# Transposes in groups of eight: TensorE's order of work in a masked attention layer, taken in steps of two units

## The chip, the cores and the metric

The kernel runs on one core of a Trainium2 chip. The time is the device time of one execution in microseconds; lower is better. Before the change it is 4194.33 us, the median of three runs (4191.17 to 4195.89 us).

## What is computed

Sixteen samples of 1024 rows by 512 columns go through one attention layer with an adjacency mask and a residual. The mask is the same for all samples and heads.

```python
h = jnp.maximum(_layernorm(x, axis=-1), 0.0)
q = (x @ Wq + bq).reshape(b, n, H, HD)      # x is h here; H = 8, HD = 64
k = (x @ Wk + bk).reshape(b, n, H, HD)
v = (x @ Wv + bv).reshape(b, n, H, HD)
scores = jnp.einsum('bihd,bjhd->bhij', q, k) / jnp.sqrt(jnp.float32(HD))
mask = jnp.where(adj == 0, jnp.float32(-1000000000.0), jnp.float32(0.0))
scores = scores + mask[None, None, :, :]
weights = jax.nn.softmax(scores, axis=-1)
out = jnp.einsum('bhij,bjhd->bihd', weights, v)
x = x + out                                  # residual, heads side by side
```

## The kernel before

**Units.** All five instruction streams are written out by hand, and semaphores join them. One sample has 8 heads and 8 blocks of 128 query rows. Its attention is cut into 128 units (`UNITS`), 64 pairs of them to 64 blocks of scores (`SBLOCKS`). A group `g` is one head with half of its query rows (four row blocks, `GB`), and the eight units of a group are its eight blocks `j` of 128 keys. For each unit `u`:

- TensorE turns four 128x128 pieces of the probabilities into one of two PSUM buffers `T` (`turn_probs`, L525). The buffer is `u % 2`.
- ScalarE copies `T` to the high part of `pT` (`probs_hi`, L633), and VectorE subtracts that copy from `T` to make the low part (`probs_low`, L796). `pT` has three buffers (`PT`). When `probs_low` is done, semaphore `p_lo` rises.
- TensorE contracts both parts with the values (`contract`, two matmuls of 512 columns, L538) into the PSUM tile `O`, which gathers over the eight units of a group. It follows its transposes by two units (`LAG = 2`).

**Scores.** On every even unit TensorE also computes a block of scores (`score`, four matmuls, L513 and L514) into one of two PSUM buffers `S`, five blocks ahead (`LEAD = 5`). VectorE adds the mask and takes the row minimum (`shift`, L790); ScalarE takes the exponential one block later (`exponential`, L641).

**The rest.** On the third unit of a group (`u % NB == LAG`, NB = 8) the group before is finished: ScalarE has copied `O` to `oT` (`copy_out`, L617), TensorE turns it into the PSUM tile `misc` (`turn_out`, L546), ScalarE copies it out (`copy_y`, L624), GpSimd scales it and adds the residual. Further work stands at numbered units (`fill`): twelve matmuls for half a projection of q or k, in two halves of six (`project_qk`, L483, at 4, 6, 8, 9, 12, 14, 16 and 17 of each 32 units), twelve for a block of the values (`project_v`, L496, at 121, 123 to 127, and 0 and 1 of the next sample), four transposes of the normalised input (`turn_h`, L462, at 83, 85, 87, 88, 91, 92, 95, 96). All of them use the one PSUM bank `misc`, which ScalarE or VectorE empties: `evacuate_qk` (L654), `bias_v` (L783), `h_high` (L669) and `h_low` (L762).

**Order on each engine.** Each engine takes its stream in the order in which it is written. ScalarE's order for unit `u` is: `copy_out` if `u % 8 == 1`, `probs_hi(u)`, the exponential if `u` is even, `copy_y` if `u % 8 == 2`, `v_high`, `evacuate_qk`, `high` (L664, the high parts of q and k, one and two units after the evacuation), `h_high`. VectorE's order is: the reciprocal (L806), `h_low`, `probs_low(u)`, `shift` of this pair's score block if `u` is even, `bias_v`, `low_q` (L772), the statistics. So on VectorE the `shift` of a pair stands between `probs_low` of its two units.

**Waits of `turn_probs`.** Unit `u` needs its PSUM buffer free, so its first transpose waits until `probs_low(u - 2)` is done. `contract(u)` waits for `probs_low(u)`.

Of the kernel before, what the change touches and what calls it, by code (L numbers as in the profile page):

```python
# [41 lines left out]
UNITS = GROUPS * NB  # L42
# [8 lines left out]
LAG = 2  # L51
# [30 lines left out]
def some(n):  # L82

    return not (isinstance(n, int) and n <= 0)


def adj_preln_kernel(nc, x, adj, Wq, bq, Wk, bk, Wv, bv, out):
    with ExitStack() as ctx:
# [98 lines left out]
        def before(b, slot, is_y, last):  # L187

            uses = []
            for s in range(slot + 1):
                if s in V_AT and not (last and s >= V_FROM):
                    nxt, j = V_AT[s]
                    uses.append((s, False, v_biased, NB * (b + nxt) + j + 1))
                if s in QK_START and not (last and QK_START[s][0] == PAIRS - 1):
                    p, k = QK_START[s]
                    uses.append((s, False, qk_evac, 4 * (PAIRS * b + p + 1) + k + 1))
                if s in HT_AT and not last:
                    uses.append((s, False, h_lo, NB * (b + 1) + HT_AT[s] + 1))  # L200
                if s % NB == LAG and some(GROUPS * b + s // NB):
                    uses.append((s, True, y_copied, GROUPS * b + s // NB))
            at = [n for n, use in enumerate(uses) if use[:2] == (slot, is_y)][0]
            if at == 0:
                return v_biased, NB * b + V_EARLY
            return uses[at - 1][2:]
# [248 lines left out]
        def _(pe):  # L455
            def turn_h(b, t, free=None, bank=misc):

                pe.wait_ge(ln_done, NB * b + t + 1)
                if free:
                    pe.wait_ge(*free)  # L460
                for c in range(C):
                    mm = pe.transpose(bank[:, c * P:(c + 1) * P], x_tile(b, t)[:, c * P:(c + 1) * P], ident[:])  # L462
                mm.then_inc(h_turned, 1)

            def project_qk(b, p, k, part, free=None, bank=misc[:]):


                w, half = 1 - k % 2, k // 2
                pair = PAIRS * b + p
                cols = slice(half * HALF, (half + 1) * HALF)  # L470
                if part == 0:
                    pe.wait_ge(h_lo, NB * (b + p // PAIRS) + GB * (half + 1))
                    if some(pair):
                        pe.wait_ge(wqk_in, 16 * pair)
                    else:
                        pe.wait_ge(w0_split, 2 if k else 1)
                    if free:
                        pe.wait_ge(*free)
                parts = [(c, wl, hl) for c in range(C) for wl, hl in ((0, 0), (0, 1), (1, 0))]
                count = len(parts) // 2  # L480
                for n in range(part * count, (part + 1) * count):
                    c, wl, hl = parts[n]
                    mm = pe.matmul(bank, wqk[:, w, c, wl, :], hT[:, hl, c, cols],  # L483
                                   start=n == 0, stop=n == len(parts) - 1)
                if part == 1:
                    mm.then_inc(qk_mm, 1)

            def project_v(b, j, free, bank=misc[:]):

                pe.wait_ge(h_lo, NB * (b + 1))  # L490
                pe.wait_ge(*free)
                if isinstance(b, int) and b == 0:
                    pe.wait_ge(wv_split, 1)
                parts = [(c, wl, hl) for c in range(C) for wl, hl in ((0, 0), (1, 0), (0, 1))]
                for n, (c, wl, hl) in enumerate(parts):
                    mm = pe.matmul(bank, hT[:, hl, c, j * P:(j + 1) * P], wv[:, wl, c, :],  # L496
                                   start=n == 0, stop=n == len(parts) - 1)
                mm.then_inc(v_mm, 1)

            def score(b, s):  # L500

                n = SBLOCKS * b + s
                q, k = qk_buffers(s // 16, (s // 8) % 2)
                i = s % NB
                pair = PAIRS * b + s // 16
                pe.wait_ge(q_low, 4 * pair + 3 + (s // 8) % 2)
                pe.wait_ge(k_copied, 64 * (pair + 1))
                if some(n - 1):
                    pe.wait_ge(exped, n - 1)
                for half in range(2):  # L510
                    cols = slice(half * HALF, (half + 1) * HALF)
                    dst = S[:, s % 2, cols]
                    pe.matmul(dst, q[:, i * P:(i + 1) * P], k[:, 0, cols], start=True, stop=False)  # L513
                    mm = pe.matmul(dst, q[:, i * P:(i + 1) * P], k[:, 1, cols], start=False, stop=True)  # L514
                mm.then_inc(scored, 1)

            def turn_probs(b, u):

                n, g, j = UNITS * b + u, u // NB, u % NB
                if j == 0:  # L520
                    pe.wait_ge(exped, GB * (GROUPS * b + g + 1))
                if some(n - 1):
                    pe.wait_ge(p_lo, n - 1)
                for i in range(GB):
                    mm = pe.transpose(T[:, u % 2, i * P:(i + 1) * P],  # L525
                                      probs[:, (GB * g + i) % RING, j * P:(j + 1) * P], ident[:])
                mm.then_inc(turned, 1)

            def contract(b, u):

                n, g, j, head = UNITS * b + u, u // NB, u % NB, u // (2 * NB)
                if g == 0:
                    pe.wait_ge(v_ready, NB * b + j + 1)
                if j == 0 and some(GROUPS * b + g):
                    pe.wait_ge(o_copied, GROUPS * b + g)
                pe.wait_ge(p_lo, n + 1)
                for part in range(2):
                    mm = pe.matmul(O[:], vs[:, j, head, :], pT[:, u % PT, part, :],  # L538
                                   start=(j == 0 and part == 0), stop=(j == NB - 1 and part == 1))
                mm.then_inc(contracted, 1)  # L540

            def turn_out(b, g, free):
                pe.wait_ge(o_copied, GROUPS * b + g + 1)
                pe.wait_ge(*free)
                for i in range(GB):
                    mm = pe.transpose(misc[:, i * P:(i + 1) * P], oT[:, i * P:(i + 1) * P], ident[:])  # L546
                mm.then_inc(o_turned, 1)

            def score_ahead(b, u, last):
                s = u // 2 + LEAD  # L550
                if u % 2 == 0 and s < SBLOCKS:
                    score(b, s)
                if u % 2 == 0 and s >= SBLOCKS and not last:
                    score(b + 1, s - SBLOCKS)

            def fill(b, u, last):
                if u in V_AT and not (last and u >= V_FROM):
                    nxt, j = V_AT[u]
                    project_v(b + nxt, j, before(b, u, False, last))
                if u in QK_START and not (last and QK_START[u][0] == PAIRS - 1):  # L560
                    p, k = QK_START[u]
                    project_qk(b, p + 1, k, 0, before(b, u, False, last))
                if u in QK_AT and not (last and QK_AT[u][0] == PAIRS - 1):
                    p, k = QK_AT[u]
                    project_qk(b, p + 1, k, 1)
                if u in HT_AT and not last:
                    turn_h(b + 1, HT_AT[u], before(b, u, False, last))
# [10 lines left out]
                score(0, s)  # L578

            def body(b, first=False, last=False):  # L580
                for u in range(UNITS):
                    if u % NB == LAG:


                        turn_probs(b, u)
                        score_ahead(b, u, last)
                        contract(b, u - LAG)
                        if u == LAG and not first:
                            turn_out(b - 1, GROUPS - 1, before(b, u, True, last))
                        if u > LAG:  # L590
                            turn_out(b, u // NB - 1, before(b, u, True, last))
                        continue
                    if u >= LAG:
                        contract(b, u - LAG)
                    elif not first:
                        contract(b - 1, UNITS - LAG + u)
                    turn_probs(b, u)
                    score_ahead(b, u, last)
                    fill(b, u, last)

            body(0, first=True)
            with pe.Fori(1, B - 1) as b:
# [290 lines left out]
```

## Time and profile before

| | us |
|---|---|
| median of three runs | 4194.33 |
| lowest, highest | 4191.17, 4195.89 |
| span of the profiled execution | 4186.6 |
| TensorE matmul busy | 4080.4 (97%) |
| VectorE busy | 3120.0 (75%) |
| ScalarE busy | 3149.6 (75%) |
| GpSimd busy | 1287.4 (31%) |

The profile is of one execution. Its span runs from the first to the last instruction. A matmul is named by the line that issues it, and its end is modelled, because matmuls overlap: a matmul of 512 columns is shown as about 0.39 us long, while the next one starts 0.23 us after it. Where a stretch is priced below, the distance between starts is used. An idle time in square brackets is that of the engine just before the instruction, with what ended it.

### The profile page before, as it was taken

Reading aid. Unit: us, or ns where it says so; the run is one execution under the profiler, and the core shown is the slowest. Engines: PE = TensorE matmul, PEld = TensorE weight load, DVE = VectorE, ACT = ScalarE, POOL = GpSimd, SP = SyncE. Lnnn points to the kernel's source line nnn. Section 1 sums busy time; section 2 is a strip of 40 time slices with the busy share of each in tenths; the row PEclk is TensorE's granted clock in tenths of the full one; section 3 lists DMA queues with packets and bytes.
Section 4 is the critical chain, followed back from the end, with each engine's and each line's share of the span. In section 5 each row is a group of like instructions: output and inputs, shape, how many; then the busy total and the mean of one; then the engine's idle time right before and its main releaser. Section 6 shows DMA issues by size and latency. Waiting matters only on the chain.

```text
span 4186.6 us, 77847 instructions
## 1 busy us (share of the span) xinstructions
PE 4080.4 (97%) x22528; PEld 3370.6 (81%) x22528; DVE 3120.0 (75%) x5128; ACT 3149.6 (75%) x5642; POOL 1287.4 (31%) x1665
## 2 busy tenths in 40 slices
PE   7999999999999999999999999999999999999998
PEld 6888888888787887878878788788887888888887
DVE  6877868778687786777867677676777768767677
ACT  5877868778687786867868688686886868868687
POOL 4233332333323333223333233332332322333222
PEclk9999999999999999999999999999999999999999
DMA  5221212212222221122212122121221212212111
GB/s 176 72 73 56 81 48 75 66 57 83 61 60 67 65 77 59 59 67 76 66 59 71 54 76 66 59 79 47 76 72 54 82 48 71 83 44 83 46 51 31
DMA packets 219598, 282.56 MB, mean 67 GB/s; under 512 B 12305, under 2 KB 143377, under 8 KB 210577
## 3 DMA queue, kind: packets, MB, share of 16 engines
q1 hardware_dynamic: 219152, 277.14, 21.9%
q8 instruction: 217, 3.56, 0.4%
q14 instruction: 229, 1.87, 0.2%
HBM read 172.23 MB, written 37.75 MB: 50 GB/s over the span
## 4 chain that ended last, share of the span: by engine, by line
PE 89%; DVE 4%; issue 3%; ACT 2%; DMA 1%; POOL 1%; DVEq 0%; SPq 0%; POOLq 0%; ACTq 0%
PE O L538 21%; PE T L525 19%; PE misc L483 17%; PE S L513 10%; PE S L514 10%; PE misc L496 8%; PE misc L546 3%; DVE pT L796 2%; PE misc L462 1%; ACT pT L633 1%; DVE qA L772 1%; DMA xln<-in_x 1%; ACT qA L664 1%; DVE S L790 1%; DVE hT L762 0%
## 5 line engine op out<-in xcount | busy, mean ns | idle before, releaser
L796 DVE TENSOR_TENSOR pT<-T,pT 128x512 fp32r<-128x512 f32 x2048 | 1412.4, 690 | 831.1 <-ACT pT L633 808.8
L633 ACT CAST pT<-T 128x512 fp32r<-128x512 f32 x2048 | 1192.7, 589 | 711.0 <-PE T L525 676.1
L538 PE MATMUL O<-pT,vs 128*128 128x512 f32 x4096 | 1366.0, 415 | 60.0 <-DVE pT L796 46.0
L790 DVE CUSTOM_DVE_ANT_0 S<-S,mask 128x1024 f32<-128x1024 f32 x1024 | 1252.3, 1223 | 5.9 <-PE S L514 4.3
L525 PEld LDWEIGHTS T<-ident,probs 128*128 128x128 f32 x8192 | 1013.9, 140 | 258.4 <-ACT probs L641 0.3
L525 PE MATMUL T<-ident,probs 128*128 128x128 f32 x8192 | 1210.1, 272 | 0.0
L641 ACT ACTIVATE probs<-S,negmax 128x1024 f32<-128x1024 f32 x1024 | 1152.6, 1126 | 8.5 <-DVE negmax L790 5.3
L538 PEld LDWEIGHTS O<-pT,vs 128*128 128x128 f32 x4096 | 690.9, 189 | 178.2 <-DVE pT L796 70.4
L483 PE MATMUL misc<-hT,wqk 128*128 128x512 f32 x3036 | 789.1, 395 | 0.0
L483 PEld LDWEIGHTS misc<-hT,wqk 128*128 128x128 f32 x3036 | 560.6, 188 | 120.3
L400 POOL TENSOR_TENSOR yparts<-yparts 128x256 f32<-128x256 f32 x256 | 188.7, 737 | 1043.9 <-ACT yparts L624 1043.2
L513 PE MATMUL S<-kA,qA 128*128 128x512 f32 x1024 | 447.2, 437 | 3.9 <-ACT probs L641 3.2
L513 PE MATMUL S<-kB,qB 128*128 128x512 f32 x1024 | 447.0, 436 | 0.0
L514 PE MATMUL S<-kA,qA 128*128 128x512 f32 x1024 | 403.3, 394 | 0.0
L514 PE MATMUL S<-kB,qB 128*128 128x512 f32 x1024 | 402.3, 393 | 0.0
L496 PE MATMUL misc<-wv,hT 128*128 128x512 f32 x1476 | 363.8, 395 | 0.4 <-issue 0.4
L377 POOL TENSOR_TENSOR vs<-proj,vs 128x512 fp32r<-128x512 f32 x128 | 168.2, 1314 | 543.4 <-ACT vs L679 543.4
L496 PEld LDWEIGHTS misc<-wv,hT 128*128 128x128 f32 x1476 | 271.2, 188 | 65.8 <-issue 6.5
L654 ACT ACTIVATE proj<-misc,bqk 128x512 f32<-128x512 f32 x253 | 174.4, 689 | 182.7 <-PE misc L483 182.7
L390 POOL TENSOR_TENSOR kA<-proj,kA 64x512 fp32r<-64x512 f32 x128 | 164.5, 1285 | 474.9 <-ACT kB L664 474.9
L513 PEld LDWEIGHTS S<-kA,qA 128*128 128x128 f32 x1024 | 193.9, 189 | 27.2 <-issue 5.7
L514 PEld LDWEIGHTS S<-kA,qA 128*128 128x128 f32 x1024 | 195.2, 191 | 21.4
(68 smaller groups left out, 3333.0 us busy)
## 6 DMA issues: line engine op xcount, KB each, us to landing
wqk<-wqk_split SPq DMA_DIRECT2D x63, 1024.0 KB, 7.0
xln<-in_x SPq DMA_DIRECT2D x240, 256.0 KB, 3.7
xres<-in_x SPq DMA_DIRECT2D x66, 512.0 KB, 3.7
kA<-kA SPq DMA_DIRECT2D x128, 256.0 KB, 3.2
kB<-kB SPq DMA_DIRECT2D x128, 256.0 KB, 3.7
out<-xres SPq DMA_DIRECT2D x64, 512.0 KB, 3.2
probs<-in_adj SPq DMA_DIRECT2D x4, 1024.0 KB, 5.1
wqk_split<-vs SPq DMA_DIRECT2D x3, 1024.0 KB, 11.0
```

Source lines behind the costliest of these rows:

```text
L400: gp.tensor_tensor(y, y, yparts[:, :, 1], ALU.add).then_inc(y_summed, 1)
L483: mm = pe.matmul(bank, wqk[:, w, c, wl, :], hT[:, hl, c, cols], start=n == 0, stop=n == len(parts) - 1)
L496: mm = pe.matmul(bank, hT[:, hl, c, j * P:(j + 1) * P], wv[:, wl, c, :], start=n == 0, stop=n == len(parts) - 1)
L513: pe.matmul(dst, q[:, i * P:(i + 1) * P], k[:, 0, cols], start=True, stop=False)
L514: mm = pe.matmul(dst, q[:, i * P:(i + 1) * P], k[:, 1, cols], start=False, stop=True)
L525: mm = pe.transpose(T[:, u % 2, i * P:(i + 1) * P], probs[:, (GB * g + i) % RING, j * P:(j + 1) * P], ident[:])
L538: mm = pe.matmul(O[:], vs[:, j, head, :], pT[:, u % PT, part, :], start=(j == 0 and part == 0), stop=(j == NB - 1 and part == 1))
L633: act.copy(pT[:, u % PT, 0, :], T[:, u % 2, :]).then_inc(p_hi, 1)
L641: act.activation(probs[:, s % RING, :], S[:, s % 2, :], ACT.Exp, bias=negmax[:, s % RING:s % RING + 1], scale=-1.0, accum_out=rowsum[:, s ...
L654: act.activation(proj[:, k % 2], bank, ACT.Identity, bias=bqk[:, w, p % PAIRS:p % PAIRS + 1], scale=-SCALE if w == 0 else 1.0).then_inc(qk ...
L790: dve.tensor_tensor_reduce(S[:, s % 2, :], S[:, s % 2, :], mask[:, s % NB, :], 1.0, 3.0e38, ALU.add, ALU.min, negmax[:, s % RING:s % RING ...
L796: dve.tensor_tensor(pT[:, u % PT, 1, :], T[:, u % 2, :], pT[:, u % PT, 0, :].bitcast(F32), ALU.subtract).then_inc(p_lo, 1)
```

## The change

Only the order of TensorE's stream in the main loop changes, by two units at a time. In a step of units `u` and `u + 1`, both `turn_probs` now come first, then both contractions (of `u - 2` and `u - 1`), then the score block, then the fills of both units. In the step where `u % 8 == 2` the order is: both `turn_probs`, the score block, `contract(u - 2)`, `turn_out`, `contract(u - 1)`, the fills. The waits inside each function, the number of instructions and the streams of ScalarE, VectorE, GpSimd and the DMA queue are as they were.

```diff
@@ body of the TensorE stream
-                for u in range(UNITS):
+                for u in range(0, UNITS, 2):
+                    turn_probs(b, u)
+                    turn_probs(b, u + 1)
+                    ended = [(b, v - LAG) if v >= LAG else (b - 1, UNITS - LAG + v) for v in (u, u + 1)]
                     if u % NB == LAG:
-                        turn_probs(b, u)
                         score_ahead(b, u, last)
-                        contract(b, u - LAG)
+                        contract(*ended[0])
                         if u == LAG and not first:
                             turn_out(b - 1, GROUPS - 1, before(b, u, True, last))
                         if u > LAG:
                             turn_out(b, u // NB - 1, before(b, u, True, last))
-                        continue
-                    if u >= LAG:
-                        contract(b, u - LAG)
-                    elif not first:
-                        contract(b - 1, UNITS - LAG + u)
-                    turn_probs(b, u)
-                    score_ahead(b, u, last)
+                        contract(*ended[1])
+                    else:
+                        if u >= LAG or not first:
+                            contract(*ended[0])
+                            contract(*ended[1])
+                        score_ahead(b, u, last)
                     fill(b, u, last)
+                    fill(b, u + 1, last)
```

TensorE's stream in the first sample, from the score block of the step of units 18 and 19 into the step of units 20 and 21, before. Here `T<-ident,probs` is `turn_probs`, `O<-pT,vs` is `contract`, `S<-` is a score block and `misc<-ident,oT` is `turn_out`.

```order
L513 MATMUL S<-kB,qB 128x512
L514 MATMUL S<-kB,qB 128x512
L538 MATMUL O<-pT,vs 128x512 x2
L546 MATMUL misc<-ident,oT 128x128 x4
L538 MATMUL O<-pT,vs 128x512 x2
L525 MATMUL T<-ident,probs 128x128 x4
L538 MATMUL O<-pT,vs 128x512 x2
L525 MATMUL T<-ident,probs 128x128 x4
L513 MATMUL S<-kB,qB 128x512
L514 MATMUL S<-kB,qB 128x512
```

The same place on TensorE after:

```order
L513 MATMUL S<-kB,qB 128x512
L514 MATMUL S<-kB,qB 128x512
L538 MATMUL O<-pT,vs 128x512 x2
L546 MATMUL misc<-ident,oT 128x128 x4
L538 MATMUL O<-pT,vs 128x512 x2
L525 MATMUL T<-ident,probs 128x128 x8
L538 MATMUL O<-pT,vs 128x512 x4
L513 MATMUL S<-kB,qB 128x512
L514 MATMUL S<-kB,qB 128x512
```

One of the two contractions that stood around a group of four transposes has moved behind both groups, and the score block now follows four contractions.

TensorE's stream around a half projection of q or k, before (the steps of units 12 and 14, `misc<-hT,wqk` is `project_qk`):

```order
L483 MATMUL misc<-hT,wqk 128x512 x6
L538 MATMUL O<-pT,vs 128x512 x2
L525 MATMUL T<-ident,probs 128x128 x4
L538 MATMUL O<-pT,vs 128x512 x2
L525 MATMUL T<-ident,probs 128x128 x4
L513 MATMUL S<-kB,qB 128x512
L514 MATMUL S<-kB,qB 128x512
L513 MATMUL S<-kB,qB 128x512
L514 MATMUL S<-kB,qB 128x512
L483 MATMUL misc<-hT,wqk 128x512 x6
```

The same place on TensorE after:

```order
L483 MATMUL misc<-hT,wqk 128x512 x6
L525 MATMUL T<-ident,probs 128x128 x8
L538 MATMUL O<-pT,vs 128x512 x4
L513 MATMUL S<-kB,qB 128x512
L514 MATMUL S<-kB,qB 128x512
L513 MATMUL S<-kB,qB 128x512
L514 MATMUL S<-kB,qB 128x512
L483 MATMUL misc<-hT,wqk 128x512 x6
```

The fill of the even unit 14 was followed by a contraction and the transposes of unit 15; those transposes now come at the head of the step, and the fill stands at its end.

## Rows read from the trace of the kernel before

**Rows 1.** Waits of all engines: who waited for whom, total us, times, longest

```profile
PE O L538 <- DVE pT L796: 46.0, 101, 0.9
```

**Rows 2.** Groups by line and shape: busy us, mean ns, idle before (TensorE, L462)

```profile
L462 PE MATMUL misc<-ident,xln 128*128 128x128 f32 x480 | 74.7, 278 | 17.7 <-POOL xln L371 10.4 <-DVE hT L762 7.2
```

**Rows 3.** Busy time by stretch: length, busy us of each engine, granted clock, DMA

```profile
1998.39:2001.11 2.72, 2.72 (x19) 2.28 (x18) 2.51 (x7) 2.28 (x4) 0.00 (x0) 1.00 0.00 0
2003.37:2007.00 3.63, 3.63 (x25) 3.06 (x24) 3.09 (x8) 3.34 (x7) 0.74 (x1) 1.00 0.00 0
2001.11:2003.37 2.26, 2.26 (x17) 1.96 (x16) 2.05 (x5) 1.98 (x4) 0.00 (x0) 1.00 0.03 7
2007.00:2011.09 4.09, 4.09 (x26) 3.42 (x24) 2.67 (x4) 2.28 (x4) 1.35 (x2) 1.00 0.37 103
```

**Rows 4.** Timeline, TensorE: start us, length us, line, tiles, count

```profile
2002.12 0.62 PE L538 MATMUL O<-pT,vs 128*128 128x512 f32 x2
2002.58 1.03 PE L525 MATMUL T<-ident,probs 128*128 128x128 f32 x8
2003.37 0.48 PE L513 MATMUL S<-kA,qA 128*128 128x512 f32 x1
...
2006.65 0.60 PE L525 MATMUL T<-ident,probs 128*128 128x128 f32 x4
2007.00 0.47 PE L513 MATMUL S<-kA,qA 128*128 128x512 f32 x1
...
2007.77 0.40 PE L514 MATMUL S<-kA,qA 128*128 128x512 f32 x1
2008.01 1.53 PE L483 MATMUL misc<-hT,wqk 128*128 128x512 f32 x6
```

**Rows 5.** Timeline, handovers between TensorE and VectorE

```profile
61.30 0.63 PE L514 MATMUL S<-kA,qA 128*128 128x512 f32 x1
...
62.11 1.23 DVE L790 CUSTOM_DVE_ANT_0 S<-S,mask 128x1024 f32<-128x1024 f32 x1 [0.41 <-PE S L514]
...
2105.11 1.22 DVE L790 CUSTOM_DVE_ANT_0 S<-S,mask 128x1024 f32<-128x1024 f32 x1
...
2106.25 0.69 DVE L796 TENSOR_TENSOR pT<-T,pT 128x512 fp32r<-128x512 f32 x1
...
4163.89 0.69 DVE L796 TENSOR_TENSOR pT<-T,pT 128x512 fp32r<-128x512 f32 x1
...
4164.63 0.73 PE L538 MATMUL O<-pT,vs 128*128 128x512 f32 x2 [0.51 <-DVE pT L796]
```

**Rows 6.** Timeline, ScalarE's copies and what they wait for

```profile
2098.68 0.69 ACT L654 ACTIVATE proj<-misc,bqk 128x512 f32<-128x512 f32 x1 [0.76 <-PE misc L483]
...
2100.31 0.60 PE L546 MATMUL misc<-ident,oT 128*128 128x128 f32 x4
...
2100.95 0.59 ACT L624 COPY yparts<-misc 128x512 f32<-128x512 f32 x1
...
2101.43 0.62 ACT L664 CAST qA<-proj 64x512 fp32r<-64x512 f32 x1
...
2101.95 0.58 ACT L633 CAST pT<-T 128x512 fp32r<-128x512 f32 x1
...
2102.56 0.69 DVE L796 TENSOR_TENSOR pT<-T,pT 128x512 fp32r<-128x512 f32 x1 [0.79 <-ACT pT L633]
```

**Rows 7.** Timeline, VectorE's bias addition behind a projection of the values

```profile
2124.81 0.69 DVE L783 TENSOR_TENSOR proj<-misc,bv_all 128x512 f32<-128x512 f32 x1 [1.14 <-PE misc L496]
```

**Rows 8.** Timeline, TensorE's longest wait near the start

```profile
58.69 0.47 PE L513 MATMUL S<-kA,qA 128*128 128x512 f32 x1 [2.02 <-ACT probs L641]
```

**Rows 9.** Busy time by stretch, behind that wait and near the end

```profile
59.00:61.00 2.00, 2.00 (x7) 1.42 (x6) 0.58 (x1) 0.72 (x2) 0.00 (x0) 0.57 1.11 344
4163.00:4178.00 15.00, 12.03 (x71) 8.85 (x68) 8.55 (x15) 8.65 (x17) 2.08 (x3) 1.00 0.00 1
```

## Prediction, made before the changed kernel was run

> **What bounds the kernel now.** I read the waits of all engines first, then the busy time of single steps, then the timeline. A step is two units; a sample has 64. TensorE almost never waits in the main loop: for the low parts of the probabilities it waited 46.0 us in the whole span [rows 1], for the normalised input 17.7 us [rows 2]. In a step with no fill ("light") it is busy for all of its 2.72 us, VectorE for 2.51 and ScalarE for 2.28 [rows 3]. So TensorE sets the time, but in light steps VectorE is close behind. A step with six fill matmuls takes 4.09, which is 1.37 more. A step with `turn_out` takes 3.63 + 2.26 - 2.72 = 3.17, since the two stretches in the group hold one such step and one light step [rows 3].
>
> **Part 1: what the grouping removes.** The switch between transposes and matmuls costs nothing that could be saved. Eight transposes together take 0.79 from start to next start (2002.58 to 2003.37), a group of four 0.35 (2006.65 to 2007.00), and four matmuls behind transposes 1.01 (2007.00 to 2008.01), against 0.46 for a pair of them behind other matmuls (2002.12 to 2002.58) [rows 4]. New light step: 0.79 + 1.01 + 0.92 = 2.72, four matmuls behind matmuls being 2 x 0.46. Old: 2.72. The gain lies within rounding, 0.01 a step or 10 us in 1024 steps; a loss of the same size is as likely. I take 0. The Trainium skill (Perfetto Trace Analysis, "Matmul Optimizations") says it is important that matmuls execute back to back in batches. By that rule the grouping would pay; the rows give it 10 us at most.
>
> **Part 2: the loop that it closes.** `T` has two buffers, so `turn_probs(u+3)`, in the next step, waits for `probs_low(u+1)`. On VectorE that stands behind `shift`, and `shift` waits for the score block of its own step. Before, `turn_probs(u+3)` was near the end of the next step, and the score block of its own step stood ahead of a contraction and a group of transposes; the loop ran over two steps and had slack. Now `turn_probs(u+3)` is near the head of the next step, and the score block comes behind both groups of transposes and both contractions. The loop has become one step long. I count from the start of `turn_probs(u+1)`:
> - 0.35 to the contractions, 1.01 for them, so the score block starts at 1.36. Its last matmul starts 3 x 0.23 later at 2.05 and ends 0.40 later [rows 4]: 2.45.
> - VectorE's `shift` starts 0.18 to 0.19 after the last score matmul's end (61.30 + 0.63 = 61.93, start 62.11) [rows 5]: 2.64. `probs_low(u+1)` starts 1.14 behind it (2105.11 to 2106.25) and takes 0.69, and TensorE starts 0.05 after its end (4163.89 + 0.69 = 4164.58, start 4164.63) [rows 5]: 4.52.
>
> `turn_probs(u+2)` is already done by then, at 2.28 + 0.43, so TensorE stands idle for 1.8 of these 4.52 us. Light step: 4.52 against 2.72, **+1.80**. What is queued behind the waiting transposes is everything else of TensorE's, so nothing else can fill the gap.
>
> **Part 3: the other steps.** The fills stand after the score block and lie in the gap as long as they are short.
> - Six fill matmuls whose result isn't taken in an even unit (units 4 and 12 of 32): covered, 4.52 against 4.09, +0.43.
> - Six whose result is evacuated at an even unit (6 and 14). ScalarE has `evacuate_qk(u)` ahead of `probs_hi(u+1)`, so `probs_hi(u+1)` waits for the fill, though its transposes are long done. The fill starts at 2.28, ends at 2.28 + 1.37 + 0.16 = 3.82 (a matmul's end lies 0.16 to 0.17 behind the next start). The evacuation starts 0.04 later, as ScalarE does behind `turn_out` (2100.91 to 2100.95), takes 0.69, of which I take 0.10 as overlapped (0.62 between starts became 0.52, 2101.43 to 2101.95) [rows 6]: `probs_hi` 4.45 to 5.04, `probs_low` 5.06 to 5.75, TensorE 5.80. **+1.71**.
> - Twelve fill matmuls (8 and 16): TensorE needs 2.72 + 2.74 = 5.46 by itself, longer than the loop, +0.
> - `turn_out` steps (2, 10, 18, 26). The score block goes ahead there, which frees `shift` early, but ScalarE has `copy_y` ahead of `probs_hi(u+1)`. Transposes 0.35, scores 1.01, one contraction 0.46: `turn_out` starts at 1.82, ends 0.60 later, `copy_y` starts at 2.47, `probs_hi` 0.52 later at 2.99, ends at 3.58, `probs_low` 3.60 to 4.29, TensorE 4.34 against 3.17: +1.17. At 10 and 18 a `high` copy lies between them (0.52 more between starts [rows 6]): 4.86, +1.69.
> - Two projections of the values in one step (124, 126 and 0): they share `misc`, and nothing stands between them any longer. The second waits for `bias_v` of the first: 0.16 to its end, 0.03 handover, 0.69 [rows 7], 0.05 = 0.93. TensorE's own sum is above the loop, so +0.93 instead of +1.80. At 120 and 122 one projection covers the loop: +0. At 2, `v_high` lies where `high` did: +1.69.
> - `turn_h` (units 83 to 96) disappears in the gap, which gives back 8 x 0.39 and its waits, 17.7/16 = 1.1. But at 88, 92 and 96 `h_high` holds up `probs_hi`, at 88 and 96 with `copy_out` too: +0.83, +0.31, +0.83. Together -2.2.
> - The old waits for VectorE, 46.0/16 = 2.9 a sample, are gone.
>
> **The sum.** Each 32 units: 6 light x 1.80 = 10.8; 2 x 0.43 = 0.9; 2 x 1.17 + 2 x 1.69 = 5.7; 2 x 1.71 = 3.4; together 20.8, four times 83.2. The values: -1.80 - 1.17 - 3 x 0.87 + 0.52 = -5.1. `turn_h` -2.2, old waits -2.9. A sample: **+73.0**. The last sample has fewer fills (more light steps, +6) and five steps with no scores, hence no loop through `shift` (-11), and none of the corrections for values and `turn_h` (+7): about +75. Sum 15 x 73 + 75 = 1170. The profiled span is 4186.6, the median 4194.33, 7.7 above it, for what lies around the span. 4194 + 1170 = 5364, **5365 us**.
>
> **Bounds of the unknown terms.** The handover to `shift` was read where the clock was low. If it is 0.04, as ScalarE's, the 25 steps a sample that go by `shift` are 0.15 shorter: -60. If the first transposes after a wait cost 0.15 more, some 51 steps a sample grow: +122. ScalarE's overlap: none instead of 0.10 on 16 steps, +26; 0.2 more, -50. Grouping itself -10 to +10. So 5240 to 5525 for this case alone.
>
> **The rivals.**
> 1. The loop is looser than I read it, because something in the step (the exponential, `copy_out`) moves so that more of it overlaps, or because the gap absorbs more in projections' steps: half of the terms at 6, 14, 10 and 18 fall away, 4 x 0.85 x 4 x 16 = -218: 5150. For it: those terms rest on long chains. Against: each of their orders is fixed in the streams.
> 2. TensorE's clock falls. After a wait of 2.02 us [rows 8] the granted clock fell to 0.57 on average of a 2 us stretch [rows 9], 1.2 instead of 2.4 GHz for most of it. The new gaps of 1.8 us are nearly that long and come in row. Against: in the last 15 us TensorE is busy for 12.03 of 15.00 with waits in each unit and keeps clock 1.00 [rows 9]. At half clock the eight matmuls in the loop take 0.23 more each and the transposes some 0.4: a light step of 6.8. If a third of the 51 waiting steps a sample is at half clock, 51 x 2.2 / 3 x 16 = +600: 5965 us. The Trainium skill (TensorE: Matmul & The Clock Gate, "HAM oscillation — how this bites in real kernels") describes kernels whose repeated waits between bursts make the clock swing; no stretch of the main loop here has such waits.
> 3. The other side, faster: the transposes, one unit earlier at every second unit, give ScalarE and VectorE more time, and the loop of part 2 does not close because `shift` comes soon enough. That is one mechanism, with its place in the light step. It decides if the way from the end of the score block to the end of `probs_low` takes less than the 0.26 us until TensorE arrives at `turn_probs(u+3)` (2.71 against 2.45). Then the old waits go (46.0 + 17.7) and 10 us of switches: 4194 - 74 = 4120. Against: 0.19 + 1.14 + 0.69 = 2.02 us [rows 5].
> 4. The change does nothing that counts, because waits merely move from one engine to another and TensorE's sum is unchanged: 4194.
>
> **How the numbers follow.** Forecast 0.76, rival 1 0.08, rival 2 0.12, rival 3 0.02, rival 4 0.02. The range takes the forecast's bounds and a little of rivals 1 and 2: 5200 to 5570. 0.2% (8 us) is about what a measurement of this kernel can tell from no change. Faster by more 0.02, within it 0.02, slower 0.96.
>
> **What would show it.** TensorE's busy share falls from 97% to about 76 to 80%. The waits gain a line "T L525 waits for pT L796" of about 1.8 us a time, some 50 times a sample, 1200 to 1400 us in total; VectorE waits for S L514 in light steps. A light step takes 4.52 us, a `turn_out` step 4.3 to 4.9, a step at 6 or 14 about 5.8, with twelve fill matmuls 5.46. Wrong would be: light steps at 2.7; a granted clock under 1 in the main loop; twelve-fill steps longer than TensorE's own sum.

## The result: 5389.73 us, 1.286 times the time before

The changed kernel takes 5389.73 us (median of 4 runs, 5388.0 to 5392.17), the kernel before 4192.75 us beside it. The ratio is 1.2856, 95% interval 1.2838 to 1.2874. The forecast was 5365, in a range of 5200 to 5570. One run further below, of the last experiment on the values, took 9753.86 us at a granted clock of 0.715 and is left out of its median.

The profile of the changed kernel. First its page: busy time and share of the span.

```profile
span 5385.9 us, 77735 instructions
...
PE 4233.6 (79%) x22528; PEld 3402.0 (63%) x22528; DVE 3143.2 (58%) x5128; ACT 3155.6 (59%) x5642; POOL 1270.1 (24%) x1665
```

TensorE was busy for 97% of the span and is now busy for 79%; its instructions are as many as before. The waits of all engines (who waited for whom, total us, times, longest) say where the rest is. VectorE's `probs_low` is now L799 and its `shift` L793, since the diff adds three lines.

```profile
DVE S L793 <- PE S L514: 1249.0, 893, 2.5
...
PE T L525 <- DVE pT L799: 1052.6, 806, 1.9
```

TensorE waits in front of the transposes 806 times, 50.4 a sample, for 1052.6 us. VectorE's `shift` waits for the score block 893 times. The first stood nowhere among the waits of before, the second with 4.3 us in 3 times; the 46.0 us at the contraction [rows 1] are down to 0.5.

The timeline of one light step, from the second group of transposes to the next such group (TensorE's weight loads, GpSimd and the DMA queue left out):

```profile
2691.87 0.66 PE L525 MATMUL T<-ident,probs 128*128 128x128 f32 x4 [1.49 <-DVE pT L799]
2692.28 1.17 PE L538 MATMUL O<-pT,vs 128*128 128x512 f32 x4
...
2693.29 0.39 PE L513 MATMUL S<-kB,qB 128*128 128x512 f32 x1
...
2693.98 0.40 PE L514 MATMUL S<-kB,qB 128*128 128x512 f32 x1
2694.21 0.60 PE L525 MATMUL T<-ident,probs 128*128 128x128 f32 x4
2694.57 1.23 DVE L793 CUSTOM_DVE_ANT_0 S<-S,mask 128x1024 f32<-128x1024 f32 x1 [0.84 <-PE S L514]
...
2695.72 0.69 DVE L799 TENSOR_TENSOR pT<-T,pT 128x512 fp32r<-128x512 f32 x1
...
2696.46 0.66 PE L525 MATMUL T<-ident,probs 128*128 128x128 f32 x4 [1.64 <-DVE pT L799]
```

This is the loop of the forecast, link by link. The score block ends at 2694.38, `shift` starts 0.19 later, `probs_low` 1.15 after that and takes 0.69, and TensorE starts its second group of transposes 0.05 behind it. It had started the first group at 2694.21 and, from that group's modelled end at 2694.81, stood idle for 1.64 us. The step takes 4.59 us.

Five steps as stretches (length, busy time of each engine, granted clock):

```profile
2691.87:2696.46 4.59, 2.95 (x17) 2.31 (x17) 3.69 (x6) 3.31 (x6) 0.59 (x1) 1.00 0.57 200
2645.86:2650.22 4.36, 3.38 (x20) 2.70 (x20) 2.64 (x6) 2.66 (x6) 1.03 (x2) 1.00 0.00 0
2654.81:2660.74 5.93, 4.31 (x22) 3.44 (x23) 2.67 (x4) 3.40 (x7) 0.00 (x0) 1.00 0.31 91
2601.59:2607.06 5.47, 5.47 (x28) 4.63 (x29) 2.61 (x5) 3.23 (x7) 2.92 (x3) 1.00 0.00 0
2430.04:2434.85 4.81, 3.33 (x22) 2.65 (x20) 2.69 (x5) 4.34 (x9) 1.37 (x3) 1.00 0.65 164
```

They are a light step, a `turn_out` step, a step with six fill matmuls that are evacuated at an even unit, a step with twelve fill matmuls, and the `turn_out` step of unit 10. They stand against 2.72, 3.17, 4.09, 5.46 and 3.17 before [rows 3]; the 5.46 is the forecast's sum for TensorE's own work, 2.72 + 2.74. Only the step with twelve is as fast as it was, and only there TensorE is busy throughout.

### The profile page after: what moved, and what is told of

The parts are those of the page before. It is cut to its first block, busy times and chain, and to the rows that moved or that the text cites. A ratio compares the mean times of both kernels' runs of the same rounds, so it can differ in the third digit from the quotient of the medians.

```text
span 5385.9 us, 77735 instructions
## 1 busy us (share of the span) xinstructions
PE 4233.6 (79%) x22528; PEld 3402.0 (63%) x22528; DVE 3143.2 (58%) x5128; ACT 3155.6 (59%) x5642; POOL 1270.1 (24%) x1665
## 4 chain that ended last, share of the span: by engine, by line
PE 68%; DVE 14%; issue 11%; ACT 6%; DVEq 1%; POOL 0%; ACTq 0%; DMA 0%; SPq 0%; POOLq 0%
PE O L538 18%; PE T L525 14%; PE misc L483 10%; DVE pT L799 10%; PE S L514 9%; PE S L513 9%; PE misc L496 6%; ACT pT L636 4%; PE misc L546 2%; DVE S L793 2%; DVE negmax L793 1%; ACT qA L667 1%; DVE proj L786 1%; ACT oT L620 0%; PE misc L462 0%
## 5 line engine op out<-in xcount | busy, mean ns | idle before, releaser
L525 PE MATMUL T<-ident,probs 128*128 128x128 f32 x8192 | 1242.6, 278 | 1069.3 <-DVE pT L799 1052.6
L793 DVE CUSTOM_DVE_ANT_0 S<-S,mask 128x1024 f32<-128x1024 f32 x1024 | 1261.7, 1232 | 1256.8 <-PE S L514 1249.0
L525 PEld LDWEIGHTS T<-ident,probs 128*128 128x128 f32 x8192 | 938.4, 140 | 1388.2 <-DVE pT L799 1247.3
L799 DVE TENSOR_TENSOR pT<-T,pT 128x512 fp32r<-128x512 f32 x2048 | 1386.2, 686 | 708.7 <-ACT pT L636 700.1
L538 PE MATMUL O<-pT,vs 128*128 128x512 f32 x4096 | 1247.3, 416 | 0.5 <-DVE pT L799 0.5
L483 PE MATMUL misc<-hT,wqk 128*128 128x512 f32 x3036 | 752.5, 390 | 0.0
L513 PE MATMUL S<-kA,qA 128*128 128x512 f32 x1024 | 416.5, 407 | 5.0 <-ACT probs L644 3.7
L513 PE MATMUL S<-kB,qB 128*128 128x512 f32 x1024 | 411.9, 402 | 0.0
L514 PE MATMUL S<-kA,qA 128*128 128x512 f32 x1024 | 407.1, 398 | 0.0
L514 PE MATMUL S<-kB,qB 128*128 128x512 f32 x1024 | 401.1, 392 | 0.0
L496 PE MATMUL misc<-wv,hT 128*128 128x512 f32 x1476 | 361.9, 394 | 44.8 <-DVE proj L786 39.4
L627 ACT COPY yparts<-misc 128x512 f32<-128x512 f32 x256 | 150.3, 587 | 267.3 <-PE misc L546 267.3
L513 PEld LDWEIGHTS S<-kA,qA 128*128 128x128 f32 x1024 | 194.3, 190 | 44.8 <-issue 6.6
```

What stands on the lines that cost most here:

```text
L525: mm = pe.transpose(T[:, u % 2, i * P:(i + 1) * P], probs[:, (GB * g + i) % RING, j * P:(j + 1) * P], ident[:])
L793: dve.tensor_tensor_reduce(S[:, s % 2, :], S[:, s % 2, :], mask[:, s % NB, :], 1.0, 3.0e38, ALU.add, ALU.min, negmax[:, s % RING:s % RING ...
L799: dve.tensor_tensor(pT[:, u % PT, 1, :], T[:, u % 2, :], pT[:, u % PT, 0, :].bitcast(F32), ALU.subtract).then_inc(p_lo, 1)
```

## Experiments

The theory is "late shift": the second group of transposes waits for `probs_low` behind `shift` behind the score block of its own step. One rival is that groups of eight transposes cost time by themselves. The other is that ScalarE's queue holds up the second `probs_hi`, since the exponential stands ahead of it.

### Scores ahead of the contractions, transposes still grouped

```diff
+                        score_ahead(b, u, last)
                         if u >= LAG or not first:
                             contract(*ended[0])
                             contract(*ended[1])
-                        score_ahead(b, u, last)
```

> The changed kernel, but in the steps without turn_out the score block stands ahead of the two contractions (transposes, transposes, scores, contractions, fills); the transposes stay grouped. Theory (late shift: the next step's second group of transposes waits for the second probs_low, which stands behind shift, which waits for the score block): the score block ends 0.92 us earlier, so a light step falls from the 4.59 us of the changed kernel's trace to 3.67, a step with six uncovered fill matmuls to TensorE's own 4.09. 17 light and 8 such steps a sample: 17 x 0.92 + 8 x 0.5 = 19.6 us, in 16 samples 315: 5075 us. Steps with an evacuation at an even unit stay at 5.94. Rival (grouping: eight transposes in a row are what costs, whatever stands behind them): 5390, unchanged. Rival (ScalarE's queue: probs_hi of the second unit comes late because of the exponential ahead of it): 5390, unchanged, since ScalarE's stream and the transposes' place are as they were.

Measured: 5133.14 us, ratio to the kernel before 1.225 (1.221 to 1.229). The light steps in the trace take 3.66 us, as expected, and those with six fill matmuls 4.09. Both rivals said "unchanged", and both fall as the cause of this part: neither the grouping nor ScalarE's stream was touched, and 257 us went. The total missed by 58 us. Some 47 of them lie in four steps a sample (units 24, 32, 56 and 64, where `u % 8 == 0`), which took 4.40 us and not 3.67; the steps with `turn_h` also gained less than a light step. A step of 4.40:

```profile
2426.17 1.08 PE L538 MATMUL O<-pT,vs 128*128 128x512 f32 x4
...
2427.30 0.59 ACT L620 COPY oT<-O 128x512 f32<-128x512 f32 x1 [1.54 <-PE O L538]
...
2427.78 1.08 ACT L636 CAST pT<-T 128x512 fp32r<-128x512 f32 x2
...
2429.15 0.66 PE L525 MATMUL T<-ident,probs 128*128 128x128 f32 x4 [1.45 <-DVE pT L799]
```

ScalarE's `copy_out` waits for the contractions, which now end 0.92 us later, and `probs_hi` stands behind it. A moved step has its price at every queue that waits for it.

### Scores at the head of every step

```diff
+                    score_ahead(b, u, last)
                     turn_probs(b, u)
                     turn_probs(b, u + 1)
```

(and `score_ahead` taken out of both branches)

> The changed kernel, but every step begins with its score block; transposes stay grouped by eight, contractions by four. Late shift: the score block leaves the way between the two groups of transposes. What is left in a light step is probs_hi, probs_low, shift and probs_low in a row behind the first group: the period P follows from 2P = 2.34 + 0.60 + 0.04 + 0.59 + 0.02 + 0.61 + 1.14 + 0.69 + 0.05, P = 3.04 us. An evacuation at an even unit then costs 4.9 instead of 5.94, a turn_out step 3.5 to 4.0 instead of 4.37 to 4.84. A sample: 17 x 1.55 + 8 x 0.5 + 8 x 1.0 + 7 x 0.87 + 8 x 0.84 + 3 x 0.9 = 54 us less, 16 samples 860: about 4530 us. Grouping theory: 5390, since the groups are the same. ScalarE's queue: 5390 less at most the few tenths that TensorE reaches the transposes otherwise.

Measured: 4664.56 us, ratio 1.113 (1.110 to 1.116). 725 of the 1197 us of loss are gone, with all transposes still in groups of eight. Grouping as the cause is ruled out for that part. It isn't for the 474 us that are left, since the kernel before has early scores too and only one group of eight in four steps; some 110 of them are the evacuation's (eight steps a sample of 4.96 us against 4.09), and how the rest divides no run shows. I had expected 4530. The light step took mostly 3.41 us from one score block to the next, instead of 3.04, because another loop bounds it, which I had not written down:

```profile
2443.62 0.50 PE L513 MATMUL S<-kA,qA 128*128 128x512 f32 x1 [0.15 <-ACT probs L643]
...
2444.65 1.03 PE L525 MATMUL T<-ident,probs 128*128 128x128 f32 x8
2445.28 0.58 ACT L635 CAST pT<-T 128x512 fp32r<-128x512 f32 x1 [1.24 <-PE T L525]
...
2445.76 1.12 ACT L643 ACTIVATE probs<-S,negmax 128x1024 f32<-128x1024 f32 x1
...
2447.03 0.50 PE L513 MATMUL S<-kA,qA 128*128 128x512 f32 x1 [0.42 <-ACT probs L643]
```

The score block needs an `S` buffer that the exponential frees; on ScalarE the exponential stands behind `probs_hi`, which waits for the transposes behind the score block: 1.03 + 0.63 + 0.48 + 1.27 = 3.41.

### The evacuation alone

```diff
-QK_SLOTS = ((4, 6), (8, 9), (12, 14), (16, 17))
+QK_SLOTS = ((4, 7), (8, 9), (12, 15), (16, 17))
```

> The changed kernel, with the second halves of the projections of q and k at units 7 and 15 instead of 6 and 14 of each 32. On TensorE the order is the same (the fill of either unit stands at the step's end); on ScalarE evacuate_qk now stands behind probs_hi of the second unit instead of ahead of it. This takes one term of the prediction by itself. If that term is right, the two steps fall from 5.94 to 4.59 us: 8 x 1.35 x 16 = -173: 5217 us. If the evacuation was hidden or only handed on to the next step: 5390.

Measured: 5298.86 us, ratio 1.265 (1.261 to 1.268), 91 us less than the changed kernel. The two steps fell from 5.93 to 4.58, as the term said; summed over the trace that is 170 us. Some of it came back. The second `high` copy moved to unit 9, ahead of `probs_hi(10)`, and from one score block to the next the `turn_out` step grew from 5.88 to 6.25 us, 8 times a sample: 45 us over the trace. GpSimd's work ran later, so TensorE's wait in front of `turn_h` grew, here in this kernel from 8.4 us to

```profile
L462 PE MATMUL misc<-ident,xln 128*128 128x128 f32 x480 | 74.7, 278 | 41.8 <-POOL xln L371 27.3 <-ACT yparts L627 14.5
```

Most of these 33 us cost nothing, because TensorE would otherwise have waited for `probs_low` in the same step. What costs more is TensorE's clock. It fell in 29 places instead of 11 (mean 0.990 instead of 0.996). The same light step (unit 20) in two samples, with the clock low in part of it and with full clock:

```profile
442.67:448.51 5.84, 4.52 (x16) 3.39 (x16) 3.44 (x6) 3.29 (x6) 1.41 (x2) 0.71 0.90 288
771.06:775.65 4.59, 2.95 (x16) 2.31 (x17) 3.45 (x6) 3.30 (x6) 1.43 (x2) 1.00 0.91 277
```

All steps with such a place together are some 46 us longer than the same steps elsewhere, against 16 us in the changed kernel. That is 170 - 45 - 30, with the rest of a few us in the `turn_h` steps, against 87 between the two traces. The term is confirmed; it can't be had by itself. Why the clock falls more often here no run shows.

### No grouping, but late scores

```diff
                         if u >= LAG or not first:
                             contract(*ended[0])
+                        turn_probs(b, u)
+                        if u >= LAG or not first:
                             contract(*ended[1])
+                        turn_probs(b, u + 1)
                         score_ahead(b, u, last)
```

(both `turn_probs` are gone from the head of the step; `turn_out` steps have the order of the kernel before)

> The other half: no grouping at all (contraction, transposes, contraction, transposes, as in the kernel before), but the score block behind them all, and the fills of both units at the step's end; turn_out steps in the old order. Late shift: the contraction of the second unit in the next step now waits for probs_low behind shift behind the late score block: 0.55 + 0.36 + 0.09 + 0.69 + 0.40 + 0.19 + 1.14 + 0.69 + 0.05 = 4.16 to 4.2 us a light step, evacuation at an even unit 5.5, turn_out steps 3.2 to 3.5: about 4870 us. Grouping theory: the groups are gone, so 4194.

Measured: 4838.23 us, ratio 1.155 (1.151 to 1.158). Here no transposes are grouped, and still 648 us are lost. A light step takes 4.17 to 4.18 us, 4.16 to 4.2 expected. The wait is the same but stands at the contraction:

```profile
2428.79 0.40 PE L514 MATMUL S<-kA,qA 128*128 128x512 f32 x1
...
2429.38 1.23 DVE L796 CUSTOM_DVE_ANT_0 S<-S,mask 128x1024 f32<-128x1024 f32 x1 [0.90 <-PE S L514]
...
2430.53 1.28 DVE L802 TENSOR_TENSOR pT<-T,pT 128x512 fp32r<-128x512 f32 x2
...
2431.27 0.74 PE L538 MATMUL O<-pT,vs 128*128 128x512 f32 x2 [1.19 <-DVE pT L802]
```

With the two runs that moved the scores this is the answer to the question of cause: grouped with early scores is faster than the changed kernel, ungrouped with late scores is slow.

### Shift behind the second `probs_low`

```diff
-                    if u % 2 == 0 and s < SBLOCKS:
+                    if u % 2 == 1 and s < SBLOCKS:
                         shift(b, s)
-                    if u % 2 == 0 and s >= SBLOCKS and not last:
+                    if u % 2 == 1 and s >= SBLOCKS and not last:
                         shift(b + 1, s - SBLOCKS)
```

> TensorE exactly as in the changed kernel; on VectorE shift stands behind the second probs_low instead of between the two. Late shift: probs_low no longer waits for the score block. The exponential comes later instead, with shift's end at 3.86 us of the step before: 2P = 3.86 + 0.04 + 1.25 + 0.60 + 0.02 + 0.69 + 0.05, P = 3.25 us a light step instead of 4.59, and 4.09 with six fill matmuls. 17 x 1.34 + 8 x 0.5 = 26.8 a sample, 430 in all: 4960 us. Grouping theory: 5390. ScalarE's queue: not faster than 5390, since the exponential comes later still.

Measured: 5102.38 us, ratio 1.218 (1.214 to 1.222). TensorE's stream is that of the changed kernel, and 287 us went by VectorE's order alone. So the link through `shift` is shown from its other end. A light step takes 3.63 us, not 3.25, and where `u % 8 == 0` it takes 4.12. The next run tells why for the 3.63.

### Both: scores ahead of the contractions, shift behind the second `probs_low`

The diffs of the first and of the last experiment together.

> The scores ahead of the contractions (light step 3.66 us in that kernel's trace) and shift behind the second probs_low (3.63 us) together, transposes grouped. Late shift: the two repairs act on different loops, the first on scores, shift, probs_low, the second leaves scores, shift, exponential, probs_hi, probs_low over two steps. Together 2P = 2 x 3.63 - 0.92, P = 3.17 us for a light step; steps with copy_out stay at 4.40, since copy_out waits for the contractions now behind the scores. Some 12 steps a sample gain 0.49 against 5133 us: about 5040 us. If one cause were behind both gains, the two together would give no more than one: 5100 or more.

Measured: 5118.66 us, ratio 1.222 (1.219 to 1.224), not 5040. My model of the light step was wrong. It takes 3.64 us with the score block early, as with the score block late:

```profile
2416.70 0.69 DVE L799 TENSOR_TENSOR pT<-T,pT 128x512 fp32r<-128x512 f32 x1 [0.31 <-ACT pT L636]
...
2417.31 1.22 DVE L793 CUSTOM_DVE_ANT_0 S<-S,mask 128x1024 f32<-128x1024 f32 x1
...
2418.63 1.12 ACT L644 ACTIVATE probs<-S,negmax 128x1024 f32<-128x1024 f32 x1 [0.90 <-DVE negmax L793]
...
2419.73 0.58 ACT L636 CAST pT<-T 128x512 fp32r<-128x512 f32 x1
...
2420.34 0.69 DVE L799 TENSOR_TENSOR pT<-T,pT 128x512 fp32r<-128x512 f32 x1 [0.31 <-ACT pT L636]
```

The loop has no TensorE in it. `shift` behind `probs_low` 0.61, the exponential 1.32 later, `probs_hi` behind it 1.10, `probs_low` 0.61: 3.64. It closes because the exponential stands ahead of the second `probs_hi` on ScalarE and `shift` behind the second `probs_low` on VectorE. So in the two kernels with `shift` moved, ScalarE's queue does bound the light step, together with VectorE's order; in the changed kernel it does not.

### Both repairs of the first kind: scores first, evacuation at odd units

The diffs of the second and of the third experiment together.

> Both repairs at once: every step begins with its score block, and the second halves of the projections stand at units 7 and 15. If the causes of the loss are separate and additive, the two steps fall from 4.9 to TensorE's own 4.09 besides: 8 x 0.84 x 16 = -107 against the kernel with scores first: about 4420 us. What would be left over the kernel before: light steps at 3.04 instead of 2.72, turn_out steps, and the pairs of value projections. If grouping itself costs something, it is over 4600.

Measured: 4684.93 us, ratio 1.118 (1.115 to 1.122), 20 us more than with scores first alone. The two gains don't add. The trace of this kernel names what took the place (TensorE's waits):

```profile
PE S L513 <- DMA kB<-kB: 76.3, 55, 1.6
PE misc L462 <- POOL xln L371: 49.9, 30, 3.8
```

With scores first alone these were 0.5 and 0.7 us. I read it so: the later `high` copies push GpSimd's subtraction and the copy of k by DMA past the time when the next pair's scores need them, and what I had called separate causes share GpSimd. The steps of units 6 and 14 did fall, to TensorE's own time, with their transposes in a group of eight:

```profile
2114.78:2118.87 4.09, 4.09 (x25) 3.46 (x24) 3.12 (x6) 2.86 (x5) 0.62 (x2) 1.00 0.33 93
```

### The two projections of the values apart

```diff
+                    elif u in V_AT and u + 1 in V_AT and not (last and u >= V_FROM):
+                        score_ahead(b, u, last)
+                        fill(b, u, last)
+                        if u >= LAG or not first:
+                            contract(*ended[0])
+                            contract(*ended[1])
+                        fill(b, u + 1, last)
+                        continue
```

> The changed kernel, except in the three steps a sample that hold two projections of the values (units 124, 126 and 0): there the order is transposes, transposes, scores, projection, contractions, projection, so that four contractions (1.01 us) stand between the two users of misc. One term of the prediction by itself: the wait of 0.88 us for bias_v (39.4 us in 45 times in the changed kernel's trace) goes, and nothing else moves, since these steps are TensorE's own: -40 us, 5350. If what the second projection waits for is handed on to the next step, 5390.

Measured: 5408.22 us, ratio 1.291 (1.289 to 1.294): 18 us slower than the changed kernel, not 40 faster. Two of the three steps lost their wait. The step of unit 0 got a longer one (in this sample the second projection's 4.42 us also fall in a place of low clock, 0.64 over 2412.50 to 2417.20; in most samples the step grew from 9.35 to some 11.2 us):

```profile
2408.74 1.07 PE L538 MATMUL O<-pT,vs 128*128 128x512 f32 x4
2409.39 0.59 ACT L644 CAST pT<-T 128x512 fp32r<-128x512 f32 x1 [8.78 <-PE O L538]
...
2411.76 0.69 DVE L794 TENSOR_TENSOR proj<-misc,bv_all 128x512 f32<-128x512 f32 x1
...
2412.50 4.42 PE L496 MATMUL misc<-wv,hT 128*128 128x512 f32 x12 [2.69 <-DVE proj L794]
```

Three `pT` buffers don't divide 128 units, so `probs_hi` of units 0 and 1 waits one contraction more than elsewhere, and that contraction now stood behind a projection. `probs_hi`, `probs_low`, `shift` and `bias_v` then ran behind it, one after the other.

### The same without the step of unit 0

```diff
-                    elif u in V_AT and u + 1 in V_AT and not (last and u >= V_FROM):
+                    elif u in (124, 126) and not last:
```

> The same order with the contractions between the two projections of the values, but only in the steps of units 124 and 126; the step of units 0 and 1 is as in the changed kernel. In the run that had it in all three steps these two fell by 0.88 us each, and the step of unit 0 grew from 9.4 to 11.2 to 12.8 us, since probs_hi of units 0 and 1 waits for the contraction of unit 126 or 127 (128 units don't divide by three pT buffers), which then stood behind the first projection. If that is all, the change is -0.88 x 30 = -26 us: about 5364. If the gain in the two steps is given back later in the sample, 5390.

Measured: 5364.06 us (median of three runs, 5361.4 to 5364.45), ratio 1.280 (1.277 to 1.282). The forecast was 5364. The wait for `bias_v` fell from 39.4 to 13.1 us, its 15 times at unit 0. The term of 0.88 us a step is real, and the loss of the run before is shown to come from the step of unit 0.

### The kernel before with a later low part of q

```diff
-LOW_AFTER = (2, 4)
+LOW_AFTER = (2, 6)
```

> The kernel before, with the second low part of q six units after the evacuation instead of four. Not about the change but about what is left in the kernel before: TensorE waited for probs_low there 0.71 and 0.18 us after each projection, behind two low_q of 0.70 to 1.1 us each in VectorE's queue. With three light steps instead of two to absorb them, the second wait (0.18, some 50 times) should go and the first stay: 4180 to 4192 us, 0 to -0.3%. Grouping plays no part in it.

Measured: 4178.82 us in 9 runs against 4190.38 in 13, ratio 0.9972, interval 0.9963 to 0.9982. It is the one version here that beats both kernels. TensorE's wait at the contraction went from 46.0 us in 101 times [rows 1] to

```profile
PE O L538 <- DVE pT L796: 37.0, 53, 0.9
```

so the second, short wait of each projection is gone and the first stayed. At units 24 and 56 most of its 0.45 us came back: the step grew by 0.35. This wait stands with the weight loads and not in the line above:

```profile
1668.74 1.37 PE L525 MATMUL T<-ident,probs 128*128 128x128 f32 x8
...
1669.45 0.42 PEld L525 LDWEIGHTS T<-ident,probs 128*128 128x128 f32 x4 [0.35 <-DVE pT L796]
```

## Why the prediction was right, point by point

| step, us | before | forecast | trace after |
|---|---|---|---|
| light | 2.72 | 4.52 | 4.59 |
| six fill matmuls, units 4 and 12 | 4.09 | 4.52 | 4.58 |
| six, evacuated at an even unit | 4.09 | 5.80 | 5.93 |
| twelve fill matmuls | 5.46 (a sum) | 5.46 | 5.47 |
| `turn_out` | 3.17 | 4.34 | 4.36 |
| `turn_out` with a `high` copy, units 10 and 18 | 3.17 | 4.86 | 4.81 |
| wait between two value projections | | 0.93 | 0.88 |

- **Part 1, grouping costs and brings nothing.** Right as far as a trace shows it, and only for TensorE's own time. In the step with twelve fill matmuls, in which TensorE never waits, the length is 5.47 against a sum of 5.46, and a step with six takes 4.09 with the group of eight (scores first, evacuation at odd units) as it did before. What the Trainium skill says of matmuls back to back in batches (Perfetto Trace Analysis, "Matmul Optimizations") found nothing to gain here: the mean granted clock before was 0.998.
- **Part 2, the loop.** Right, and shown from both ends: by moving the score block on TensorE (5133, 4665), by moving `shift` on VectorE (5102), and by the late score block with no grouping (4838).
- **Mis-sized by a little.** The first transposes behind a wait take 0.41 us up to the next start (2691.87 to 2692.28), not the 0.35 of [rows 4]. With 806 waits that is 48 us. I had this as an unknown of 0 to 0.15 and took 0. The evacuation is 0.13 dearer than I said, 0.06 of it the same; in its trace it starts 0.12 behind the fill's modelled end, not 0.04. With some 126 such steps that is 9 us. The last sample grew by 83 us instead of 75, and the clock took 16 us (see below).
- **An error the other way, and some luck.** The waits of before were taken out at 46.0 us. But such a wait is counted from the modelled end of the transposes, 0.24 behind the next start (0.60 against 0.36), and a step with one was longer by more than the wait. Two light steps of the kernel before, with waits of 0.71 and 0.17 us, took 6.89 us together and not 2 x 2.72 = 5.44:

```profile
1667.17:1670.90 3.73, 3.02 (x17) 2.32 (x16) 3.65 (x6) 2.76 (x5) 0.00 (x0) 1.00 0.89 334
1670.90:1674.06 3.16, 2.99 (x18) 2.31 (x17) 3.01 (x5) 2.26 (x5) 0.00 (x0) 1.00 0.09 33
```

That is 0.28 more for each of 101 waits, an estimate of 28 us that the change also took away. So terms of 48, 9, 8 and 16 us stood against 28 and some I have not sought; that the total missed by only 25 us is in part luck.

- **The handover of 0.19 to `shift`.** It was read where the clock was low and holds at full clock too (2694.38 to 2694.57).
- **"1.8 us a time" of waiting.** The number of waits was right (50 a sample), their size not: 1.31 on average, 1052.6 in total instead of 1200 to 1400. In light steps the profile shows 1.64, since it counts from a matmul's modelled end, 0.16 behind the next start; and steps with fills or `turn_out` wait less, which I had not averaged in.
- **Rival 1, a looser loop.** The `turn_out` and evacuation steps have their full length; it falls.
- **Rival 2, the clock.** It came, but small: 16 us and not 600. The prediction had named a granted clock under 1 in the main loop as a sign of being wrong, and that sign did show; see below.
- **Rivals 3 and 4** fall with the sign.

What failed were seven of the ten expectations of experiments, by 58 to 265 us. Five failed for one reason: I followed the loop that I was cutting and not the next one. Behind the first lay `copy_out` (4.40 us), behind the second the `S` buffers through ScalarE (3.41), behind the third, in two runs, VectorE and ScalarE without TensorE (3.64), and at unit 0 the `pT` buffers. The two with the evacuation at odd units failed because the work that moved with it held up something else (the `turn_out` steps, GpSimd) and, in the first of them, because the clock fell more often.

## What to carry to other kernels

Before steps of one in-order engine are regrouped, write for each wait how many steps its loop spans. A wait that had a whole step of slack can lose it without any instruction being added, and the cost is then the sum of the handovers around the loop, on all engines, not the busy time of one. Once a loop is cut, work out the next one before counting the gain.

## What the runs showed of the hardware that I had not expected

TensorE's clock fell now and then in the changed kernel, although it was busy for 79% of the time: in eleven short stretches of the 16 samples, all in the steps of units 90 and 98; the mean is 0.996. One such place, behind three waits of 1.80, 1.21 and 1.94 us:

```profile
2310.63 1.04 PE L525 MATMUL T<-ident,probs 128*128 128x128 f32 x4 [1.94 <-DVE pT L799]
2311.32 0.78 PE L513 MATMUL S<-kA,qA 128*128 128x512 f32 x1
2311.89 0.63 PE L514 MATMUL S<-kA,qA 128*128 128x512 f32 x1
```

The step of unit 98 as a stretch in this sample; in the next sample it is the `turn_out` step of 4.36 us shown with the result:

```profile
2310.63:2316.58 5.95, 4.97 (x20) 3.91 (x20) 2.64 (x6) 2.66 (x6) 1.03 (x2) 0.71 0.00 0
```

The granted clock over 2310.63 to 2314.03 is 0.52, the level of 1.2 GHz, and at 2315.00 four transposes take 0.60 us again. Behind the waits of 1.64 us in a row in the light steps of this kernel the clock stayed at 1.00. So the rival that priced this at 600 us had its mechanism but the wrong frequency: the eleven steps are 0.9 to 1.6 us longer than the same steps in other samples, some 16 us in all.

The other thing is how exactly such loops add up: 1.32 + 1.10 + 0.61 + 0.61 for 3.64 us, and 1.03 + 0.63 + 0.48 + 1.27 for 3.41, from rows of single instructions.
